# A fused attention and mixture-of-experts kernel: the order of GpSimd's four passes in the joint stage, and when they start

## The reference

```python
q = _ln(latents, sa_ln_g, sa_ln_b)
x = latents + _mha(q, q, sa_in_w, sa_in_b, sa_out_w, sa_out_b)
qc = _ln(x, ca_q_ln_g, ca_q_ln_b)
kv = _ln(tokens, ca_kv_ln_g, ca_kv_ln_b)
x = x + _mha(qc, kv, ca_in_w, ca_in_b, ca_out_w, ca_out_b)
return _fuse_moe(x, moe_ln_g, moe_ln_b, router_w, router_b, fc1_w, fc1_b, fc2_w, fc2_b)
```

## Time and profile before

| | us |
|---|---|
| median of 3 runs | 1674.48 |
| lowest and highest | 1670.7, 1675.24 |
| the profiled execution's own time | 1682.22 |
| its span, first to last instruction | 1680.4 |

### The profile page before, as it was taken

How to read it: one execution, slowest core, us unless ns; L and a number is a source line. 1 busy time by engine, 2 the same in 40 slices (tenths; PEclk the granted TensorE clock), 3 DMA queues, 4 the chain that set the end, 5 groups by cost and what they waited for, 6 DMA issues and landing times. The chain is left out here.

```text
span 1680.4 us, 29040 instructions
## 1 busy us (share of the span) xinstructions
PE 1451.7 (86%) x9973; PEld 750.6 (45%) x9974; DVE 1189.7 (71%) x1725; ACT 843.4 (50%) x1709; POOL 741.6 (44%) x465
## 2 busy tenths in 40 slices
PE   5996999999999999999548889863499999999996
PEld 3551222222222222222323445432388887888885
DVE  4758999999999999994366776425666565655653
ACT  2332888888888888888214445430032222222221
POOL 1005999999910000000131321110258876888784
PEclk8996999999999999999767878665599999999998
DMA  3577455564513112000455656445623322233231
GB/s 120 189 219 214 144 152 139 162 196 144 160 49 95 32 32 84 2 1 1 143 103 121 152 122 124 96 104 203 261 41 54 61 53 46 53 57 54 54 57 17
DMA packets 134790, 172.68 MB, mean 103 GB/s; under 512 B 30008, under 2 KB 100089, under 8 KB 134187
## 3 DMA queue, kind: packets, MB, share of 16 engines
q1 hardware_dynamic: 107499, 119.26, 26.6%
q0 software_dynamic: 27200, 52.24, 12.8%
HBM read 102.09 MB, written 66.25 MB: 100 GB/s over the span
## 5 line engine op out<-in xcount | busy, mean ns | idle before, releaser
L1118 DVE TENSOR_REDUCE sa_half_maxs<-sa_psm 128x2 f32<-128x1024 f32 x512 | 604.4, 1221 | 32.1 <-PE sa_psm L983 23.5
L1102 ACT ACTIVATE sa_p<-sa_pss 128x512 f32<-128x512 f32 x1024 | 532.9, 604 | 90.5 <-PE sa_pss L1026 90.3
L1026 PE MATMUL sa_pss<-sa_q,sa_k 49*128 49x512 f16 x1024 | 312.2, 385 | 7.7
L1041 PE MATMUL sa_pso<-sa_p,sa_v 128*32 128x512 f32 x2048 | 274.4, 608 | 18.8 <-ACT sa_o L1079 9.4
L2320 ACT ACTIVATE moe_h<-moe_psh,moe_b 128x256 f32<-128x256 f32 x312 | 122.2, 474 | 332.4 <-PE moe_psh L2257 332.4
L983 PE MATMUL sa_psm<-sa_k,sa_q 48*128 48x512 f16 x1024 | 259.7, 393 | 13.1 <-DVE sa_half_maxs L1118 12.8
L1026 PEld LDWEIGHTS sa_pss<-sa_q,sa_k 49*128 49x128 f16 x1024 | 77.7, 94 | 320.5 <-ACT sa_p L1102 265.2
L2255 PE MATMUL moe_psh<-moe_hh,w_high 128*128 128x256 f16 x624 | 172.8, 277 | 0.0
L1391 POOL TENSOR_TENSOR x_xb<-x_xb,early_bo 128x1024 f32<-128x1024 f32 x4 | 9.5, 2378 | 370.0 <-DMA x_xb<-in_x 370.0
L2256 PE MATMUL moe_psh<-moe_hl,w_high 128*128 128x256 f16 x624 | 172.8, 277 | 0.0
L2257 PE MATMUL moe_psh<-moe_hh,w_low 128*128 128x256 f16 x624 | 172.6, 277 | 0.0
(11 more groups left out here) (205 smaller groups left out, 2047.8 us busy)
## 6 DMA issues: line engine op xcount, KB each, us to landing
sa_w_stage<-in_w POOLq DMA_DIRECT2D x32, 512.0 KB, 5.4
dram_sa_v<-qkv_v_sb SPq DMA_DIRECT2D x8, 1024.0 KB, 5.3
dram_sa_qk_parts<-qkv_part SPq DMA_DIRECT2D x16, 512.0 KB, 6.7
sa_v<-dram_sa_v SPq DMA_DIRECT2D x16, 512.0 KB, 5.8
dram_w_high<-sa_w_high POOLq DMA_DIRECT2D x32, 256.0 KB, 2.7
dram_w_low<-sa_w_low POOLq DMA_DIRECT2D x32, 256.0 KB, 3.1
dram_sa_raw<-sa_o SPq DMA_DIRECT2D x4, 2048.0 KB, 8.8
w_high<-dram_w_high SPq DMA_DIRECT2D x16, 512.0 KB, 15.2
```

The source lines that it names most:

```text
L1026: pe.matmul(ps_s[place % SBANKS][:], k_st[u][rows, j0 + j, kt * kp:(kt + 1) * kp], q_st[u][rows, j0 + j, half * HALF:(half + 1) * HALF], s ...
L1041: mm = pe.matmul(ps_o[h * VW:(h + 1) * VW, :], v_st[u][:, kt, v_at:v_at + VW], probs[n % PSLOTS][h][:], start=(kt == 0), stop=(kt == key_t ...
L1102: act.activation(probs[n % PSLOTS][h][:], ps_s[place % SBANKS][:], ACT.Exp, scale=float(DH) ** -0.5).then_inc(read, 1)
L1118: dv.tensor_reduce(half_maxs[U % 2][:, at % 2, :, c], ps_m[z][:], AX_X, ALU.max).then_inc(taken, 1)
```

## The change

GpSimd's loop gets another order and another shift. In step t it first waits for the third pair of fills of block t - 2; `biased_x` and `normed_o1` are done for block t + 1 in place of t; `normed_o2` stands ahead of `biased_x1`.

```diff
                 for t in range(STEPS):
-                    biased_x(t)
-                    normed_o1(t)
+                    if here(t - 2):
+                        pool.wait_ge(filled, PAIRS * (t - 2) + 3)
+                    biased_x(t + 1)
+                    normed_o1(t + 1)
+                    normed_o2(t - 4)
                     biased_x1(t - 2)
-                    normed_o2(t - 4)
```

## The result

The changed kernel takes 1750.5 us (1749.0 to 1753.4), the one before 1674.9 in the same comparison: 1.0436 times as long, 95% interval 1.040 to 1.047. The profiled execution has a span of 1751.6 us against 1680.4, 71.2 more; the last normalising group of the joint stage starts at 1216.0 instead of 1143.6 us, 72.4 later, so the stage holds all of it.

What follows compares the result with a forecast made beforehand. No engine is full; a chain passing between engines bounds each step. Stalls less collision losses make step 7 63.0 us late, 5 more for the clock: 68; 1674.5 + 68 = 1742.5, say 1743 us, range 1724 to 1764.

Steps and rivals of the forecast that it cites:

- its signs in the profile: Steps 2 to 7: residual1 waits for the bias sum, some 88 us; normalising takes 1.4 us; steps grow to 48 us.
- The bias sum moves behind a load that lands in the middle of the step: GpSimd's bias sum on x1 stands behind x(t+1)'s load, stalling VectorE's first residual add, some 88 us over steps 2 to 7.
- The wait on the fills costs nothing: GpSimd's new wait on the third fill: that fill ends at about the first residual add, the load lands later; no cost.
- The sum step by step: Start of each joint-stage step's first residual add, worked out through steps 2 to 7: 63.0 us late at step 7.
- R(2) to R(7): Starts of VectorE's first residual add in steps 2 to 7; forecast from 871.2 to 1083.0 us.
- an undisturbed R to row, from step 7, ... 13.25: Time from a step's first residual add to its negated row, read from step 7 before the change: 13.25 us.
- What the clock adds: 0 to 10, I take 5: TensorE's lower granted clock after idling delays work from the third step on: 0 to 10 us in all, 5 taken.
- the fills and reductions after the stall wait for VectorE anyway: Reason given for taking 5 of 0 to 10 us for the low clock after TensorE's stall.
- The load is there in time: Rival: x(t+1) lands by the first residual add, 47.5 us of stall less losses, some 26, 1700 us; chance 0.09.
- TensorE at the low clock becomes a chain of its own: Rival: the negated row itself slips 2 to 3 us in each of five steps, some 86, 1760 us; chance 0.10.
- VectorE's reductions set the pace after R: Argument against the low-clock rival: after the first residual add, VectorE's reductions set the pace; no size given.
- The losses go and the new wait hides: Rival: VectorE reaches residual1 only after GpSimd's burst, so only collision losses vanish: 16.5 us faster, 1658 us; chance 0.03.

Runs made afterwards that it cites:

- An edit: Changed kernel with 18, 22, 23 and 7 extra matmuls of 128 rows in 32 bit in TensorE's stall of steps 4 to 7: 1747.3 us, ratio 1.040.
- the last kernel: Kernel before, with o2's product first, GpSimd's other three passes after a normalising, bias sum one step early, no fill wait: 1660.9 us, ratio 0.988.

## Why the prediction was right

The forecast was 1743 us with a range of 1724 to 1764, and slower by 4.1%; measured were 1750.5 and 4.4%. Its mechanism, its chain and its signs in the profile are found, and so are both signs that it gave for a size that is off: the way from the residual add to the row was 15 us and not 13, and the loads of x(5) to x(7) landed 23.1, 26.0 and 26.8 us behind the row, where 24 to 26 had been given. By the spans of the profiled executions the miss is 3.2 us, 71.2 against 68. The rest of the 7.5 us comes from the median beside which the sum was put, 1674.5 us: in all later comparisons the kernel before had a median of 1678.9 us or more.

- *The bias sum moves behind a load that lands in the middle of the step.* Shown by the order of the passes alone: with the bias sum and the product on o2 ahead of the load the loss is gone (ratio 1.001), with the bias sum alone ahead of it three quarters of residual1's waits are. Predicted waits: 12, 11, 19, 20, 20 and 6 us, 88; measured 11.7, 11.6, 18.4, 22.7, 23.5 and 9.5, 97.4.
- *The wait on the fills costs nothing.* Shown: without it 1753.4 us, ratio 1.043 against 1.044. That holds as long as the load is late; with the load early it is what the burst waits for.
- *The sum step by step.* R(2) to R(7) were forecast at 871.2, 906.8, 951.7, 1000.3, 1048.8 and 1083.0; they came at 870.8, 904.7, 949.4, 999.6, 1051.0 and 1088.3, and the stage itself started 0.7 us later than before. The step that was mis-sized is "an undisturbed R to row, from step 7, ... 13.25": it was 14.9, 15.3 and 15.3 us in steps 4 to 6, 5.8 us in all, where that step 7 ran at a granted clock of 0.96 and these at about 0.6. Most of the excess, 1.2 to 1.6 us a step, is VectorE's wait for TensorE's row (the brackets that name L1491 in its rows after), which it did not have in that step 7. Behind it the chain from the row on came longer too, 26.8 against 25.8 in step 5 and 17.4 against 16.2 in step 6, and step 7 to the end of the stage another 4.1 (72.4 - 68.3). Up to R(3) the sum had been 2.1 us too long, which hid part of it: half of that is the undisturbed way from add to normalising, 9.05 us in step 2 and not the 10.0 that was taken. That the total came so near is in part this luck.
- *What the clock adds: 0 to 10, I take 5.* The size was set too low by a few us; "the fills and reductions after the stall wait for VectorE anyway" is where it went wrong, as out2 and the turned row do not: the first half of out2 took 3.78 us in step 5, and 2.00 in step 7 before. An edit shows the clock as the cause in one step only, 13.47 against 15.26 us. The other traces agree with it. In steps 4 to 7 of all kernels above, as far as no GpSimd pass lengthens VectorE's instructions, no late product on o2 and no extra work holds TensorE back, the way from the residual add to the row is 12.4 to 13.5 us in the seven stretches with a granted clock of 0.87 or more, and 14.2 to 15.8 us in all those at 0.77 or less. The stall itself is not needed for it: in the last kernel, where residual1 waits at most 1.8 us, it is 12.40 us at 1.00 and 15.07 at 0.77. What the clock costs in the whole kernel stays open.
- *The rivals.* "The load is there in time" was made to happen: 1714.5 us, not the 1700 worked out; the stall was 58.6 us and not 47.5. "TensorE at the low clock becomes a chain of its own" came true in part: the row slips by 1.7 to 2.1 us in steps 4 to 7, where it had 2 to 3 us in each of five steps, so "VectorE's reductions set the pace after R" holds only up to the normalising. "The losses go and the new wait hides" was made to happen with another order: 1660.9 us against the 1658 worked out, which is 16.5 below; measured are 21.2 (1682.1 beside it). The total fits better than its terms. From one residual add to the next, steps 1 to 6 became 5.9, 4.7, 1.5, 3.4, 2.2 and 7.3 us shorter, where 2.0, 4.05, 3.3 and three times 2.4 had been put down, and from step 7 to the end of the stage 4.3 us were lost again. In step 1 the variance is hit as well (residual add to normalising 9.69 us before, 5.45 in that kernel), which the prediction did not count, as it counted only 3.36 against 1.38.

## What to carry to other kernels

Before an operation is put later in an in-order engine's loop, look at what stands in front of it, and when the latest of those waits ends: here one 2.35 us pass, moved behind a load that lands 10 us into the step, cost 10 to 23 us a step, because the other engine's first instruction waits for it. Put what the next engine needs first, and what needs the late transfer last. A pass that collides with another engine can be tied to an event of that engine (here VectorE's last normalising) in place of one that merely tends to come at the right time; the one version here that does so is 1.2% faster than the kernel before.

## What was not expected of the hardware

Matmuls of 48 rows by 77 columns, issued without a gap for 20 us, did not hold TensorE's granted clock: it was 1.00 in the stretch in which they began and 0.50 (1.2 GHz) in the later ones of the same stall, the value that the stretch has when TensorE is idle in it, while matmuls of 128 rows in 32 bit ran through 36 us at 1.00 (2.4 GHz). Busy time in the profile and a full clock are thus not the same thing. The two kinds of matmul differ in rows and in type; which of the two matters no run here tells. After the dense matmuls the clock fell again during the step's own fills and scores, to a mean of 0.77 in step 5 and 0.87 in step 6.
